# The bias of an attention's output projection: added by GpSimd to the centred rows instead of by two products of ones with the bias

## What is computed

```python
x = x + attn_ref(layernorm(x), ...)   # layer 1, "fast weights"
x = x + ffn_ref(layernorm(x), ...)    # layer 2
```

```python
h = rmsnorm(x, attn_norm_w); qkv = h @ qkv_w + qkv_b      # 16 query heads, 4 kv heads, 64 wide
q, k = rope(q), rope(k)
y = causal attention over a window of 128, with a sink per head
x = x + (y @ proj_w + proj_b)
h2 = rmsnorm(x, ffn_norm_w)
topv, topi = top_k(h2 @ gate_w + gate_b, 4)               # 4 of 32 experts, softmax of topv
y2 = sum over the chosen experts of weight * (silu(h2 @ wg) * (h2 @ wu)) @ wd
return x + y2
```

## Time and profile before

| | us |
|---|---|
| median of three runs (lowest to highest) | 962.77 (962.35 to 964.63) |
| the profiled execution | 962.39 |
| its span, first to last instruction | 960.6 |
| TensorE busy | 836.1 (87% of the span) |
| VectorE busy | 754.0 (78%) |
| ScalarE busy | 595.3 (62%) |
| GpSimd busy | 478.6 (50%) |

### The profile page before, as it was taken

The page is one execution under the profiler, slowest core; times in us unless marked ns, Lnnn a source line. Parts: engine busy times, 40 slices in busy tenths (PEclk is TensorE's granted clock), DMA queues, the critical chain, the costliest instruction groups (busy, mean ns, idle before and its releaser), DMA issues. The chain is left out here.

```text
span 960.6 us, 21474 instructions
## 1 busy us (share of the span) xinstructions
PE 836.1 (87%) x6518; PEld 642.3 (67%) x6586; DVE 754.0 (78%) x2735; ACT 595.3 (62%) x1915; POOL 478.6 (50%) x609
## 2 busy tenths in 40 slices
PE   1788999999999999999999999999983699999700
PEld 0445677777777777777777777777661588888600
DVE  2647979889898898989989899888865477777618
ACT  0114877868788687877878778687761465664300
POOL 1213223545555456554555554556437167777740
PEclk9799999999999999999999999999996799999955
DMA  6879999999940000000000000000001454444149
GB/s 163 265 240 374 375 374 375 370 369 367 369 131 20 7 20 20 10 23 8 19 17 11 19 14 20 13 14 26 19 17 42 114 140 129 127 132 114 53 137 334
DMA packets 97346, 129.41 MB, mean 135 GB/s; under 512 B 14513, under 2 KB 54354, under 8 KB 97234
## 3 DMA queue, kind: packets, MB, share of 16 engines
q1 hardware_dynamic: 84690, 108.36, 34.4%
q0 software_dynamic: 8192, 17.58, 5.5%
q10 hardware_dynamic: 4352, 2.10, 0.7%
HBM read 30.34 MB, written 97.65 MB: 133 GB/s over the span
## 5 line engine op out<-in xcount | busy, mean ns | idle before, releaser
L1331 POOL TENSOR_TENSOR l_t_cos<-l_t_cos,l_t_sin 128x512 f32<-128x512 f32 (+1 forms) x96 | 114.6, 1194 | 226.1 <-DVE l_t_sin L910 225.9
L1164 ACT ACTIVATE l_prob<-l_score,l_nm 128x128 f32<-128x128 f32 (+1 forms) x512 | 212.5, 437 | 19.0 <-DVE l_nm L770 18.8
L1552 POOL DMA_INDIRECT expert_out<-e_yo,e_dest x128 | 122.7, 958 | 59.8 <-issue 32.9
L94 POOL DMA_INDIRECT expert_rows<-h,slot x128 | 130.0, 1016 | 40.2 <-issue 33.7
L1174 ACT COPY l_probT<-l_turned 128x512 f32<-128x512 f32 x192 | 111.4, 593 | 58.6 <-PE l_turned L392 57.6
L759 DVE TENSOR_REDUCE l_mx<-l_score 128x2 f32<-128x512 f32 (+1 forms) x192 | 123.2, 683 | 24.1 <-PE l_score L378 22.8
L392 PEld LDWEIGHTS l_turned<-ident_sb,l_prob 128*128 128x128 f32 x768 | 87.6, 141 | 49.7 <-issue 42.4
L1164 ACT ACTIVATION_READ_ACCUMULATOR l_prob<-l_score,l_nm 128x1 f32 x512 | 113.2, 221 | 0.0
L392 PE MATMUL l_turned<-ident_sb,l_prob 128*128 128x128 f32 x768 | 111.1, 278 | 1.8 <-DVE l_prob L744 1.0
L378 PE MATMUL l_score<-l_kT,l_qT 64*128 64x128 f32 (+1 forms) x1024 | 109.8, 343 | 0.0
L407 PE MATMUL l_turned<-l_probT,l_vv 128*64 128x128 f32 x1536 | 105.0, 279 | 1.4 <-ACT l_probT L1174 1.4
(11 more groups left out here) (274 smaller groups left out, 1719.2 us busy)
## 6 DMA issues: line engine op xcount, KB each, us to landing
expert_rows<-zeros SPq DMA_DIRECT2D x32, 2240.0 KB, 22.6
e_xt<-expert_rows SPq DMA_DIRECT2D x160, 70.0 KB
e_yo<-expert_out SPq DMA_DIRECT2D x16, 512.0 KB, 5.8
wup_sb<-in_wup SPq DMA_DIRECT2D x1, 4096.0 KB, 15.1
expert_rows<-zeros SPq DMA_DIRECT2D x32, 70.0 KB, 2.3
expert_rows<-zeros SPq DMA_DIRECT2D x4, 560.0 KB, 12.0
expert_rows<-h,slot POOLq DMA_INDIRECT x128, 2.4
expert_out<-e_yo,e_dest POOLq DMA_INDIRECT x128
```

The lines of the kernel that those rows point to most:

```text
L94: m["nc"].gpsimd.indirect_dma_start(m["xs"], bass.IndirectOffsetOnAxis(ap=m["slot"][:, par, c:c + 1], axis=0), m["h2"][:, par, c // TOPK, ...
L1164: ins = A_.activation(prob[:, b, h, cols], score[(2 * u + h) % 3][:, cols], ACT.Exp, bias=nm[:, b, h, j:j + 1], scale=0.125, accum_out=sum ...
L1331: g.tensor_tensor(t_cos[:, c % 2, 0:w], t_cos[:, c % 2, 0:w], t_sin[:, c % 2, 0:w], ALU.add).then_inc(s["added"], 1)
L1552: g_.indirect_dma_start(m["ys"], bass.IndirectOffsetOnAxis(ap=dest[:, t:t + 1], axis=0), yo[:, t, :], None).then_inc(sent[t % GROUP], 16)
```

## The change

The two products of ones with the bias (one for each token tile of a sequence) are taken out of TensorE's list, and the first product of each accumulation starts it instead. The bias is spread over 128 rows once, in iteration 1, together with the gate's: the product in `idle` and VectorE's copy are 160 columns wide instead of 32. GpSimd adds it to the centred rows `xx` in place, 128x256 in one instruction, in each iteration between send 0 and send 1. `attended` waits for this addition in place of the centred rows.

```diff
@@ -278,7 +278,8 @@
         wexp, wrec = sb("wexp", [P, TPS, TOPK]), sb("wrec", [P, TPS])
         hot, prod = sb("hot", [P, TPS, TOPK, EXPERTS]), sb("prod", [P, TPS, TOPK, EXPERTS])
         picked, place = sb("picked", [P, TPS, EXPERTS], BF16), sb("place", [P, TPS, EXPERTS])
-        gate_b = sb("gate_b", [P, EXPERTS])
+        late_b = sb("late_b", [P, D + EXPERTS])
+        proj_b, gate_b = late_b[:, 0:D], late_b[:, D:]
         h2, slot, sent = m["h2"], m["slot"], m["sent"]
         score = [ps(f"score{i}") for i in range(3)]
         turned = [ps(f"turned{i}") for i in range(2)]
@@ -293,7 +294,7 @@
             "s_ps mx nm es_in es_out exped den rec normed t_ps probT y_ps yT "
 
             "proj_ps xx x2 ss rms2 h2 h2_ps h2T gate_ps glog top w_in wexp wrec idx idxf hot picked rank_ps "
-            "place prod masksum slotf slot x_sum").split()
+            "place prod masksum slotf slot x_sum xx_b").split()
         s = {n: ctx.enter_context(nc.semaphore("l_" + n)) for n in names}
         block = ctx.enter_context(nc.Block())
 
@@ -351,9 +352,6 @@
         @block.tensor
         def _(pe):
             mm, tr = nc.tensor.matmul, nc.tensor.transpose
-
-            def bias(dst, c0, c1):
-                mm(dst, m["ones_bf"][:], m["bias3"][:, c0:c1], start=True, stop=False)
 
             def scores(n, par, u):
                 A, ap, u, done = at_unit(n, par, u)
@@ -576,10 +574,8 @@
                     after(pe, s["place"], B)
 
                 pe.wait_ge(s["yT"], B * UNITS + (2 if t else 3) + 3 * k)
-                if k == 0:
-                    bias(side_g[:, cols], QKV, QKV + D)
                 for p in range(4 * k, 4 * k + 4):
-                    ins = mm(side_g[:, cols], yT[:, par, p, cols], m["wproj"][:, p, :], start=False,
+                    ins = mm(side_g[:, cols], yT[:, par, p, cols], m["wproj"][:, p, :], start=(p == 0),
                              stop=(p == PAIRS - 1))
                 ins.then_inc(s["proj_ps"], 1)
 
@@ -632,7 +628,7 @@
                         mm(score[k][:], m["ones"][:], m["wqkv"][:, cols], start=True, stop=False)
                         mm(score[k][:], m["ones_bf"][:], m["bias3"][:, cols], start=False, stop=True) \
                             .then_inc(s["fold_ps"], 1)
-                    mm(turned[1][:, 0:EXPERTS], m["ones_bf"][:], m["bias3"][:, QKV + D:QKV + D + EXPERTS],
+                    mm(turned[1][:, 0:D + EXPERTS], m["ones_bf"][:], m["bias3"][:, QKV:QKV + D + EXPERTS],
                        start=True, stop=True).then_inc(s["fold_ps"], 1)
                 elif n == SEQS + 3:
                     keep_clock(1, score[2])
@@ -923,7 +919,7 @@
                 B = n - 4
                 if not live(B):
                     return
-                v.wait_ge(s["xx"], TPS * B + TPS)
+                v.wait_ge(s["xx_b"], B + 1)
                 after(v, s["x_sum"], B)
                 v.wait_ge(s["proj_ps"], 4 * B + 4)
 
@@ -1014,7 +1010,7 @@
                                            in1=m["wqkv"][:, cols], op0=ALU.mult, op1=ALU.subtract).then_inc(s["folded"], 1)
                     if u == 10:
                         v.wait_ge(s["fold_ps"], 4)
-                        V.tensor_copy(gate_b[:], turned[1][:, 0:EXPERTS]).then_inc(s["folded"], 1)
+                        V.tensor_copy(late_b[:], turned[1][:, 0:D + EXPERTS]).then_inc(s["folded"], 1)
                 if n != 0:
                     return
                 if u == 3:
@@ -1352,6 +1348,15 @@
                 pool.wait_ge(s["small"], O * 6 + 6)
                 g.tensor_tensor(rms[:], sq[:], rs[:], ALU.mult).then_inc(s["norms"], 1)
 
+            def centred_bias(n, par):
+                B = n - 4
+                if not live(B):
+                    return
+                if B == 0:
+                    pool.wait_ge(s["folded"], 5)
+                pool.wait_ge(s["xx"], TPS * B + TPS)
+                g.tensor_tensor(xx[:], xx[:], proj_b[:, None, :].broadcast_to([P, TPS, D]), ALU.add).then_inc(s["xx_b"], 1)
+
             def rms2(n, par):
                 B = n - 4
                 if not live(B):
@@ -1403,6 +1408,7 @@
 
             def iteration(n, par):
                 send(n, par, 0)
+                centred_bias(n, par)
                 send(n, par, 1)
                 rope_add(n, par, 2)
                 rms2(n, par)
```

## The result

The changed kernel took 967.43 us (median of 8 runs, 965.98 to 970.22) against 963.27 us for the kernel before in the same session: 1.0043 times as long, 95% interval 1.0027 to 1.0059. So it is 4.2 us slower, where 1.3 us faster was forecast. The prediction was 961.5 us; the time lies above its range, on the side of the slower rival. The profiled execution took 965.98 us with a span of 964.2 us, 3.6 us longer than the one before.

The account below looks back on a forecast made before the run. TensorE's queue was taken to bound the kernel; -1.32 - 0.48 - 0.25 + 0.6 + 0.1 + 0.1 = -1.25 us gave 961.1 from the profiled 962.39, forecast as 961.5 on the runs' median scale, range 957.9 to 967.

Parts of the forecast that it names:

- the slower rival: Addition runs behind all four scalings; TensorE waits 0.6 to 0.9 us in 12 iterations, 968.5 to 972.5 us; chance 0.16.
- What bounds the kernel: Attention loop, iterations 4 to 15: TensorE's queue sets the time, busy 39.73 to 39.78 of each 40 us.
- what goes: TensorE's 32 bias products: per full iteration 0.11 us saved at token tile 0, 0.04 at tile 1.
- The addition, the scatters, L1331: GpSimd, full iterations: addition at 421.2, last two scatters some 1.0 us later, L1331 at 424.4, no cost.
- The step that failed: VectorE in full iterations: L814 would run ahead of L1331 instead of behind it, 0.8 us sooner.
- the tightest place, 0.18 us: TensorE's load of the next rotation addition's result, chunk 3: slack 0.18 us, claimed to get looser.
- The tail: Last iteration: TensorE waits for normed rows behind GpSimd's queue; the later scatters cost 0.6 us, ends +0.9 and -1.4.
- its point of decision: On GpSimd in full iterations: the slow case holds once the addition starts later than about 421.55.
- the wait it expected at chunk 2: TensorE would wait for L1331's result 0.6 to 0.9 us in each of 12 iterations.

Follow-up runs that it names:

- run 1: Changed kernel without GpSimd's bias addition, so only the removal of the bias products is left: 961.26 us, 0.9987 of the kernel before, period 40.47 us.
- run 9: Changed kernel with VectorE's L810 reading its SBUF operand once instead of twice: 1.0048 of the kernel before, period 40.99 us.
- run 6: Kernel before with GpSimd's addition put in at the changed kernel's place, bias products kept: 1.0041 of the kernel before, period 41.07 us.
- run 4: Changed kernel with VectorE's centring moved earlier and GpSimd's addition in its idle time before the scatters: 960.71 us, 0.9983 of the kernel before.
- run 5: Changed kernel with VectorE's L810 moved ahead of its copy L808: 1.0081 of the kernel before, period 41.36 us.
- run 3: Changed kernel with the fourth scatter moved behind the rotation's addition of chunk 2: 0.9994 of the kernel before, period 40.55 us.
- run 2: Changed kernel with GpSimd's addition replaced by a memset on an unused tile: 1.0071 of the kernel before, period 41.16 us.
- run 8: Changed kernel with GpSimd's addition cut to one token tile, 128x128 instead of 128x256: 1.0019 of the kernel before, period 40.74 us.

## Why the prediction was wrong

- **What bounds the kernel, what goes:** right. 0.11 and 0.04 us per iteration, and the waiting load behind tile 1 is where the rest stays (run 1).
- **The addition, the scatters, L1331:** right to 0.1 us. The addition gets in behind the first scaling and holds the second; VectorE's rotation is 0.03 us later.
- **The step that failed:** "But L814 at 424.1 now runs ahead of L1331 instead of behind it, 0.8 us sooner." I moved L1331 back past L814 and gave L814 the time that it takes alone. But what stood in L1331's place was not nothing: it was the end of the fourth scatter. L814 comes up 0.2 us ahead of that scatter's end in six of eleven iterations and 0.01 to 0.02 in the others, is held, and L1331 is served first when the scatter ends. So L814 moved back with L1331 by 0.55, instead of forward. The trace of the kernel before had such a hold, in L748 (behind run 9); the prediction took the hold by an addition from it and not the one by a scatter.
- **What hung on it:** the prediction called chunk 3 "the tightest place, 0.18 us" and said that it gets looser. It got tighter by 0.58 us and turned into a wait of TensorE in each iteration: 0.58 - 0.18 = 0.40 us longer, which is the period's 41.02 against 40.62. Most of the saving of 0.15 is hidden in that wait (run 6).
- **The sum:** the 11 periods from iteration 4 to 15 put L427 3.9 us back against L429 before. The changed kernel had come to iteration 4 0.5 us early, in a stretch where the changed lines hardly run (runs 1 and 4 lie between 0.2 late and 0.8 early there). At the last iteration's first scatter it is 3.35 us late (719.58 against 716.23), with the tail 3.9, and the experts' block gives 0.3 back: 3.6 us of span.
- **The tail:** right. From the first scatter of the last iteration to the first of the experts' block it is 17.39 us before and 17.91 after: +0.5, forecast +0.6.
- **The slower rival** came nearest in time, but not by what happened: its point of decision, an addition that starts past 421.55, was not reached (421.04), and the wait it expected at chunk 2 is not there.
- The Trainium skill ("SBUF — State Buffer", "Who interferes with whom") has the rule that I weighed, one lock for a pair of ports, held for whole instructions, and also says that what GpSimd does for a DMA that it issues needs those ports. I drew the first half into the sum and not the second. The runs agree that such a DMA and VectorE get in each other's way, with three differences. The page tells of the DMA that waits for VectorE, and here VectorE waits. It says that a `tensor_tensor` does not stall such a DMA and infers that the two need different halves of the pair; L748 is one and was held all the same (0.99 us instead of 0.69). And L810 was issued 0.2 us ahead of L1327 and still came second, though the page lets issue order decide.

Open: why L810 loses to L1327 at the scatter's end, while in the kernel before the product L748 at 449.08 (0.99 us) got in ahead of L1374 in the same position. One of the ten periods is 0.35 us longer (41.37) in all kernels that have the addition, or the memset, at that place. In that iteration VectorE's L721 (L725 before), ahead of the centring, starts 0.35 us later than in the others, in the kernel before too (379.83, 10.14 us behind the start of L429 instead of 9.80). There the slack takes it up; where the addition waits for the centred rows, the scatters and L810 come later by as much. What delays L721 the traces do not show.

## What to carry to other kernels

When an instruction is moved back, ask what fills the place it leaves and whether that holds the same neighbours; here the end of a scatter held L814 where the rotation's addition had held it before, so the victim moved along with its holder. A late engine is paid for at the next tight slack, not where it is late, so follow it to there. An added operation on a lightly loaded engine is not free because the engine often waits; it was free in idle time with nothing queued close behind it: the same addition some 5 us earlier, ahead of the scatters, cost nothing (run 4).

## What the runs showed of the hardware

- An indirect DMA on GpSimd (0.96 us) held VectorE's instructions between SBUF tiles that started in its second half, until its end: a scaling that starts 0.05 us into it takes its usual time, one that starts 0.58 into it ends 0.09 behind the scatter (run 1); L748 takes 0.69 us from 0.15 into it and 0.99 from 0.67 into it (before). It holds with one read as with two (runs 9 and 5), but not for every instruction: the squares L929, with two reads, start 0.70 us into a scatter and take their usual 0.29 (run 3).
- A GpSimd memset, which only writes, holds such a VectorE instruction too: the four scalings took 1.70 us beside a memset of 0.89, and 1.26 without (run 2 and the earlier trace rows).
- An f32 addition on GpSimd costs 0.49 us for 128x128 (run 8) and 0.72 to 0.76 for 128x256 (run 4, the changed kernel); by my estimate from these, some 0.2 of it does not depend on the size.
